# Own buffers and a later place for the last rope group of an attention layer

## The reference, cut to what matters

```
re = te * c - to * s          # rope: even and odd channels, turned
ro = te * s + to * c
scores = q . k * scale;  attn = softmax(scores);  out = attn . v
```

## Time and profile before

| | us |
|---|---|
| median of three runs | 903.22 (901.86 to 906.53) |
| the profiled execution | 900.48 |
| its span in the trace | 898.7 |
| TensorE busy | 860.2 (96%) |
| ScalarE busy | 682.0 (76%) |
| VectorE busy | 675.0 (75%) |
| GpSimd busy | 616.5 (69%) |

### The profile page before, as it was taken

How to read it: one execution, slowest core, us unless ns; L and a number is a source line. 1 busy time by engine, 2 the same in 40 slices (tenths; PEclk the granted TensorE clock), 3 DMA queues, 4 the chain that set the end, 5 groups by cost and what they waited for, 6 DMA issues and landing times.

```text
span 898.7 us, 16917 instructions
## 1 busy us (share of the span) xinstructions
PE 860.2 (96%) x5128; PEld 498.8 (56%) x5128; DVE 675.0 (75%) x1063; ACT 682.0 (76%) x1111; POOL 616.5 (69%) x438
## 2 busy tenths in 40 slices
PE   8999789999999999999999978999999999999995
PEld 5568344445444454458786733445444454446874
DVE  1879987888888888863577987888888888884455
ACT  2744789999999999971453489999999999995142
POOL 0318867888878888881344786788878887786135
PEclk8999999999999999999999999999999999999998
DMA  9865999999898899996201699999899999998101
GB/s 243 236 241 119 181 205 176 173 196 173 162 193 169 169 186 174 168 179 217 94 24 36 153 191 194 179 178 191 163 175 187 169 171 191 172 174 181 61 1 48
DMA packets 423964, 145.82 MB, mean 162 GB/s; under 512 B 408220, under 2 KB 416240, under 8 KB 423152
## 3 DMA queue, kind: packets, MB, share of 16 engines
q1 hardware_dynamic: 423152, 142.91, 78.2%
q0 software_dynamic: 608, 2.10, 0.7%
q10 hardware_dynamic: 160, 0.26, 0.1%
HBM read 23.85 MB, written 7.60 MB: 35 GB/s over the span
## 4 chain that ended last, share of the span: by engine, by line
PE 71%; DVE 8%; SPq 5%; ACT 4%; POOL 4%; issue 4%; DMA 4%; DVEq 0%; ACTq 0%; POOLq 0%
PE Tb L1269 18%; PE OO L1240 13%; PE Sa L1240 12%; PE Sb L1240 8%; PE Ta L1251 5%; PE Sa L1387 3%; PE Sb L1387 2%; SPq L369 2%; SPq L338 2%; DMA PT_dma<-P_parts 1%; PE Sb L1279 1%; ACT probs L633 1%; POOL turned L442 1%; DVE QO L1023 1%; PE OO L1129 1%
## 5 line engine op out<-in xcount | busy, mean ns | idle before, releaser
L468 POOL TENSOR_TENSOR P_parts<-probs,P_parts 128x768 f16<-128x768 f32 x256 | 419.9, 1658 | 106.5 <-ACT P_parts L526 106.4
L526 ACT ACTIVATE P_parts<-probs 128x768 f16<-128x768 f32 x256 | 205.6, 842 | 6.5 <-DMA PT_dma<-P_parts 5.2
L926 DVE TENSOR_TENSOR PT_lo<-Ta,PT_hi 128x512 f16<-128x512 f32 x128 | 88.5, 691 | 62.5 <-ACT PT_hi L526 60.0
L902 DVE TENSOR_REDUCE small<-OO 128x1 f32<-128x1024 f32 x96 | 117.1, 1220 | 21.4 <-PE OO L1240 21.4
L1269 PE MATMUL Tb<-PT_dma,V_hi 128*64 128x512 f16 x768 | 132.1, 385 | 0.0
L633 ACT ACTIVATE probs<-OO,small,scales 128x1024 f32<-128x1024 f32 x96 | 115.4, 1202 | 18.3 <-DVE small L905 16.7
L1240 PE MATMUL OO<-K_hi,Q_parts 128*128 128x512 f16 x384 | 115.5, 383 | 10.1 <-ACT probs L633 8.3
L902 DVE TENSOR_REDUCE small<-Sa 128x1 f32<-128x1024 f32 x96 | 116.9, 1217 | 8.4 <-PE Sa L1240 8.4
L1240 PE MATMUL Sa<-K_hi,Q_parts 128*128 128x512 f16 x384 | 115.9, 384 | 3.6 <-ACT probs L633 3.6
L633 ACT ACTIVATE probs<-Sa,small,scales 128x1024 f32<-128x1024 f32 x96 | 115.6, 1204 | 4.9 <-DVE small L905 2.5
L902 DVE TENSOR_REDUCE small<-Sb 128x1 f32<-128x1024 f32 x64 | 77.9, 1218 | 12.1 <-PE Sb L1240 12.1
(11 more groups left out here) (303 smaller groups left out, 1551.7 us busy)
## 6 DMA issues: line engine op xcount, KB each, us to landing
Q_parts<-turned_parts SPq DMA_DIRECT2D x64, 128.0 KB, 2.4
TT<-ternary SPq DMA_DIRECT2D x2, 2304.0 KB, 8.4
Q_parts<-Q_parts SPq DMA_DIRECT2D x16, 256.0 KB, 3.1
PT_dma<-P_parts SPq DMA_TRANSPOSE x256, 3.9
ternary<-tern SPq DMA_DIRECT2D x1, 2304.0 KB, 9.9
wo<-in_L_attn_w_o_dram SPq DMA_DIRECT2D x4, 512.0 KB, 9.7
xq<-in_L_attn_x_dram SPq DMA_DIRECT2D x2, 1024.0 KB, 10.6
wq_low<-Wq_lo SPq DMA_DIRECT2D x1, 2048.0 KB, 14.3
```

The lines of the kernel that those rows point to most:

```text
L468: nc.gpsimd.tensor_tensor(P_parts[:, n % DEEP, 1, :], probs[n % DEEP][:, KP * P:S], P_parts[:, n % DEEP, 0, :], ALU.subtract).then_inc(par ...
L526: return nc.scalar.activation(o, i, ACT.Copy, scale=scale)
L902: nc.vector.tensor_reduce(nmax[:, n % 4:n % 4 + 1], scores_bank(n)[:, :], AX.X, ALU.max, negate=True).then_inc(row_max, 1)
L926: nc.vector.tensor_tensor(PT_lo[place].rearrange("p k (t q) -> p t k q", t=2), T_BANK[:, :].rearrange("p (t k q) -> p t k q", t=2, k=KP), ...
```

## The change

The last group gets buffers of its own, `turned_end` and `parts_end`, in the place of `Wq_lo`. GpSimd's additions for it wait for the last query product in place of the low parts of the group before. VectorE's cast and subtraction for it move from the steps 0 and 2 to the steps 8 and 12 of the first pair, with no wait for earlier moves. SyncE moves its two latent parts in front of the transposes 9 and 10, and its rope parts in front of 13 and 15; at tile 8 SyncE waits for the moves of the first three groups alone, and in front of the first prefetch for all of them. TensorE waits for these moves in the middle pairs (1 to 6), at step 14, and no longer in the first.

```diff
+        (turned_end, parts_end), AT = lay(
+            K_AT - H * 2 * P * 4, ("turned_end", [P, 2, S], F), ("parts_end", [P, 2, 2, S], F16))
+        assert AT <= K_AT
...
                 def rotary_moves(g, j):
+                    parts = parts_end if g == GROUPS - 1 else turned_parts
...
                     for i in range(2):
                         t = 4 * g + 2 * i
-                        sp.wait_ge(lat_lo, b * 4 * GROUPS + 4 * g + 2 * i + 2)
-                        sp.dma_start(Q_parts[64:128, t, :, :], Q_parts[0:64, t + 1, :, :]).then_inc(lat_moved, 16)
+                        if g < GROUPS - 1:
+                            sp.wait_ge(lat_lo, b * 4 * GROUPS + 4 * g + 2 * i + 2)
+                            sp.dma_start(Q_parts[64:128, t, :, :], Q_parts[0:64, t + 1, :, :]).then_inc(lat_moved, 16)
...
-                        if first and n in (3, 5):
+                        if first and n == 8:
+                            for j in range(2):
+                                sp.wait_ge(turned_out[j], (b + 1) * 64 * GROUPS - 64)
+                        if first and n in (9, 10):
+                            t = 4 * (GROUPS - 1) + 2 * (n - 9)
+                            sp.wait_ge(lat_lo, (b + 1) * 4 * GROUPS)
+                            sp.dma_start(Q_parts[64:128, t, :, :], Q_parts[0:64, t + 1, :, :]).then_inc(lat_moved, 16)
+                        if first and n in (13, 15):
                             sp.wait_ge(lat_moved, (b + 1) * 32 * GROUPS)
-                            rotary_moves(GROUPS - 1, n // 2 - 1)
-                        if first and n == 8:
-                            sp.wait_ge(lat_moved, (b + 1) * 32 * GROUPS)
-                            for j in range(2):
-                                sp.wait_ge(turned_out[j], (b + 1) * 64 * GROUPS)
+                            rotary_moves(GROUPS - 1, n // 2 - 6)
...
                 sp.wait_ge(wvo_out, 16)
+                for j in range(2):
+                    sp.wait_ge(turned_out[j], (b + 1) * 64 * GROUPS)
                 for c, end in enumerate((2, 4, 6, PAIRS)):
                     prefetch(c)
...
-                        if g >= 1:
+                        if g == GROUPS - 1:
+                            pool.wait_ge(q_ps, (b + 1) * 4 * GROUPS)
+                        elif g >= 1:
                             pool.wait_ge(rope_lo[j], b * GROUPS + g)
-                        nc.gpsimd.tensor_tensor(turned[:, j, :], qmul[:, 2 * j, :], qmul[:, 2 * j + 1, :],
+                        nc.gpsimd.tensor_tensor((turned_end if g == GROUPS - 1 else turned)[:, j, :], qmul[:, 2 * j, :], qmul[:, 2 * j + 1, :],
...
                 def rotary_parts_high(g, j):
                     dve.wait_ge(rope_sum, b * 2 * GROUPS + 2 * g + j + 1)
-                    dve.wait_ge(turned_out[j], b * 64 * GROUPS + 64 * g)
-                    nc.vector.tensor_copy(turned_parts[:, j, 0, :], turned[:, j, :]).then_inc(rope_hi, 1)
+                    nc.vector.tensor_copy(parts_end[:, j, 0, :], turned_end[:, j, :]).then_inc(rope_hi, 1)
+
+                def last_parts_low(j):
+                    dve.wait_ge(rope_hi, (b + 1) * 2 * GROUPS - 1 + j)
+                    nc.vector.tensor_tensor(parts_end[:, j, 1, :], turned_end[:, j, :], parts_end[:, j, 0, :],
+                                            ALU.subtract).then_inc(rope_lo[j], 1)
...
-                        if first and n in (0, 2):
-                            rotary_parts_high(GROUPS - 1, n // 2)
+                        if first and n in (8, 12):
+                            rotary_parts_high(GROUPS - 1, n // 4 - 2)
                         transposed_low(pair * (TILES // 2) + n // 2, n + 1)
-                        if first and n in (0, 2):
-                            rotary_parts_low(GROUPS - 1, n // 2)
+                        if first and n in (8, 12):
+                            last_parts_low(n // 4 - 2)
...
-                        if first and n == TILES - 2:
+                        if not (first or last) and n == TILES - 2:
                             pe.wait_ge(lat_moved, b * 32 * GROUPS + 32 * GROUPS)
```

More of the change, by code:

```diff
@@ L338, in rotary_moves @@
                         sp.dma_start(Q_parts[32 * j:32 * j + 32, 4 * g + s, :, :],
-                                     turned_parts[32 * s:32 * s + 32, j, :, :]).then_inc(turned_out[j], 16)
+                                     parts[32 * s:32 * s + 32, j, :, :]).then_inc(turned_out[j], 16)
                 for g in range(GROUPS):
```

## The result

The kernel after takes 908.14 us in the median of eleven runs (904.70 to 913.66), the kernel before in the same session 903.04 (eleven runs, 898.75 to 906.53): a ratio of 1.0064, 95% interval 1.0045 to 1.0083, which is 4 to 7.5 us slower. The forecast, 906.3 us and most likely no change that a measurement can tell, lies on the right side and 1.8 us under the median, inside its range. Of its three outcomes it held no change beyond 0.5% the likeliest (0.53, against 0.36 for slower by more); the measured 0.64% lies past that line, with an interval that reaches to both sides of it. How much of that is its terms being right, and how much errors that cancel, is what the rest is about.

What follows compares the result with a forecast made beforehand. TensorE was taken to set the end, losing time only by waiting and slow clock in each batch's opening 40 us. Gains of 6.1 against 9.2 paid gave 3.1 us slower, 906.3 us on the 903.22 median; range 899.5 to 911.5.

Steps and rivals of the forecast that it cites:

- What is removed: First eight tiles of the first pair: ScalarE's waits go, 2.7 us in the second batch and 3.4 in the first.
- third rival: First eight tiles not shortened as said, tile 7 being held by its bank: 910.8 us, chance 0.08.
- Tile 8's step, 2 x 2.0: First pair, tile 8: cast and rope subtraction wait for GpSimd, tile 13's exponent comes 2.0 us later in each batch.
- first rival: VectorE finds the ports free, ahead of GpSimd, in both batches: 904 down to 899.7 us, chance 0.25.
- Tile 12's step, 2 x 1.6: First pair, tile 12: tile 17's maximum 1.9 us later, moves and prefetch delay transpose 16; TensorE loses 1.6 each batch.
- The clock, 2 x 1.0: TensorE's gaps before the scores of tiles 7 and 15: one clock fall charged per batch, 1.0 us each.
- second rival: Low clock follows both gaps, before tiles 7 and 15, in both batches, and the prefetch slows transpose 16: 910.1 us, chance 0.23.
- The small terms: Moves at tiles 9 and 10 lie in SyncE's idle time; TensorE's three waits in six middle pairs: taken as 0.
- The sum: Whole kernel: 6.1 us gained, 9.2 paid, net 3.1 slower, 906.3 us on the median of the runs.

Runs made afterwards that it cites:

- filled gaps: After plus fourteen identity transposes on TensorE ahead of the scores of tiles 7 and 15, first pair: 901.73 us, 1.0029 of before.
- low on GpSimd: After with the two rope subtractions on GpSimd, behind its subtractions of tiles 9 and 13, instead of VectorE: 913.04 us, 1.012 of before.
- moves later: After with the last four moves and the first prefetch put off into and behind the second pair: 908.11 us, 1.0085 of before.
- second pair: After with parts made in the second pair, eight moves singly before its transposes 8 to 15, first prefetch behind: 910.5 us, 1.0094 of before.
- GpSimd with moves spread: Low on GpSimd, but eight moves before every fourth transpose of second and third pair, first prefetch behind: 902.55 us, 1.0009 of before.
- second pair spread: Parts made in the second pair, but eight moves before every fourth transpose of third and fourth pair: 901.24 us, 1.0014 of before.
- buffers only: After with VectorE's and SyncE's order as before; new buffers, GpSimd's wait and TensorE's waits stay: 901.36 us, 0.9988 of before.
- parts early: After with VectorE's casts and subtractions back at steps 0 and 2; own buffers and SyncE's late moves stay: 915.62 us, 1.0153 of before.
- the kernel of the third pair: Against second pair spread: casts in third pair, subtractions on GpSimd, moves over fourth and fifth, prefetches later, tile 7's gap filled: 896.53 us, 0.9940 of before.

## Why the prediction was right, point by point

- **What is removed.** The waits went as said. 6.1 us were counted; where no clock fell (filled gaps), 4.1 + 3.3 = 7.4 were gained by tile 12. The opening's worth was under-sized by 1.3. The third rival, that nothing would be gained, is refuted.
- **Tile 8's step, 2 x 2.0.** Tile 12 to tile 13 costs 2.4 and 2.3 in the table, in every kernel that subtracts there on VectorE, and exponent 8 to exponent 13 went from 11.64 and 11.35 to 13.36 in both batches, 1.7 and 2.0 more. The cast waits for GpSimd and the subtraction ends 1.1 behind it, as walked. The Trainium skill, page "SBUF — State Buffer", section "Who interferes with whom", has it that the order of issue decides who stands still: here VectorE came second with its cast and both subtractions, by 0.3 to 0.6 us, and paid. The one GpSimd subtraction that came second (553.37) paid too. So the first rival, that VectorE comes first, was not met.
- **Tile 12's step, 2 x 1.6.** Right in kind, under-sized. Tile 17's exponent loses 1.8 in both batches where no clock falls, as walked (1.9). But tile 20's transpose adds more than the 0.3 given to it: without falls, tile 13 to tile 24 costs 2.3 and 2.8 in place of 1.6. The order was as walked (moves, prefetch, transpose 16), but the prefetch came 1.0 later and the transpose 0.7 (570.96 and 572.25, less the 2.51 by which tile 0 is later in after's trace, against 567.4 and 569.0), and the cast of tile 20 waited 1.48.
- **The clock, 2 x 1.0.** This is the step that failed: "I charge one of the two in each batch". The price of one fall was right, 0.9 to 1.2 us of the path for the two gaps. The count was not: in after's profile both gaps of both batches were followed by a fall, and so was a third gap in the second batch, which the late transpose opened and which cost 1.6; no term stood for that one. By tile 24 they have cost 1.6 and 3.6 (after less filled gaps: 2.2 less 0.6, 5.4 less 1.8), 5.2 in place of 2.0. That is the second rival's mechanism, forecast at 910.1. What the count was read from, the length of a gap, doesn't decide it. Gaps of 2.56 us before tile 7's scores stand twelve times in the profiles of six kernels (after, low on GpSimd, moves later, second pair, GpSimd with moves spread, second pair spread), and the clock fell behind six of them. Gaps of 3.15 us and more there stand six times (before, buffers only, parts early), with four falls. Behind the fourteen such gaps that transposes filled there was none. So one fall for two gaps is near the mean of the first kind, and the profiled execution had more. The other ten runs of after have no trace; their mean granted clock, 0.980 to 0.991 against 0.986 in the profiled one, goes with their times (913.66 us at 0.980, 904.70 at 0.991), so the count may well differ between them.
- **The small terms.** The new buffers, GpSimd's wait and TensorE's waits cost nothing that can be told: the kernel with only these is at 0.9988 of before. The moves at tiles 9 and 10 are not in it; they are in the kernel of the third pair, which has lost nothing by tile 13 (-4.1 / -3.2).
- **The sum.** 7.4 gained, 4.7 at tile 8, 5.1 at tile 12 and 5.2 for the clock make 7.6, which is what the table has at tile 24 (2.2 + 5.4). The forecast had 3.1: the gain was taken too small by 1.3 and the loss by 5.8 (15.0 against 9.2). Of the executions profiled, that of before lies 2.6 under its median (900.48, 903.04) and that of after 0.5 over (908.68, 908.14), so between medians it is 5.1. The sign and the places of gain and loss were derived; that 906.3 is so near to 908.14 owes something to errors of both signs.

What the prediction walked through but did not price by itself is SyncE's order, the larger danger. It counted a transpose 0.3 us late beyond VectorE's lateness; with that cover gone SyncE's order, with the low clock that follows it, costs 6 to 7 us a batch (parts early less buffers only, tile 24).

## What to carry to other kernels

Work that is moved out of a stage bounded by chains with a slack of one tile should go to a stage in which the bounding engine is busy throughout and the engine that takes the work idles, not to the next stretch of the same kind: the same parts cost about 5 us a batch in the second eight tiles (filled gaps, tile 12 to 24), and 0.1 up to tile 80 when made in the third pair and moved in the two after it. (Made in the second pair with VectorE alone they still cost 2.3 and 3.3 by tile 32; whether it was the pair or GpSimd's share of the work that made the difference was not tried apart.) A queue that issues in order is an engine like the others: set the issue time of what is put between its regular entries against their period. And when an experiment removes one late engine and the time gets worse, look for what that engine was hiding before giving up the theory.

## What the runs showed of the hardware that was not expected

- The granted clock doesn't follow from the length of a gap alone: behind gaps of 2.56 and 2.36 us it fell in one batch and not in the other of the same execution (moves later), behind 2.15 (filled gaps) it did not fall where it fell behind 2.14 (after), and behind 3.17 and 3.15 (parts early) it did not fall where it fell behind 3.15 in before.
- A fall in the granted clock can be free: removing it in before changed nothing (0.9998), and in after it was worth 3 to 5 us.
- A move on SyncE was issued every 0.7 us in a run of four, and took 0.6 to 1.8 us where it stood alone between two transposes (second pair).
- A prefetch of output weights in front of the last pair or inside it went with a loss of 0.4 to 2.3 us a batch behind tile 112, in all seven kernels that have it there.
